# Second attention of a two-layer transformer: searches and sort one slot on with three near buffers, and ScalarE's exponential between its two counts

## The reference, cut to what matters

```
B, T, D, H = x.shape[0], 1024, 128, 16      # as run: x is (4, 1024, 128)
topk = max(1, int(Tx * 0.3))
scale = Dx ** (-0.5)
...
scores = jnp.einsum('bhid,bhjd->bhij', q, k) * scale
topk_scores, indices = jax.lax.top_k(scores, topk)
...
masked = jnp.full_like(scores, -jnp.inf)
masked = masked.at[bi, hi, ti, indices].set(topk_scores)
attn = jax.nn.softmax(masked, axis=-1)
out = jnp.einsum('bhij,bhjd->bhid', attn, v)
```

## Time and profile before

| | |
|---|---|
| median of 3 runs | 3562.24 us (3561.92 to 3563.55) |
| the profiled execution | 3559.1 us |
| its span | 3557.4 us |
| busy share of the span: PE, DVE, ACT, POOL | 77%, 76%, 70%, 56% |
| mean granted TensorE clock | 0.787 of full speed |
| second attention, about | 1050 us to 3120 us of the span |

### The profile page before, as it was taken

How to read it: one execution, slowest core, us unless ns; L and a number is a source line. 1 busy time by engine, 2 the same in 40 slices (tenths; PEclk the granted TensorE clock), 3 DMA queues, 4 the chain that set the end, 5 groups by cost and what they waited for, 6 DMA issues and landing times. The chain is left out here.

```text
span 3557.4 us, 74747 instructions
## 1 busy us (share of the span) xinstructions
PE 2733.3 (77%) x23705; PEld 1525.9 (43%) x23705; DVE 2690.0 (76%) x8588; ACT 2479.6 (70%) x4051; POOL 1983.9 (56%) x4543
## 2 busy tenths in 40 slices
PE   4699999677745777777777776776777777757999
PEld 2233333233423445454444454453445545444444
DVE  5787787235439989999999989897999999834444
ACT  2266666433128999999999999997999999822222
POOL 3133333410228888888888888886888888730000
PEclk8699999888655777777777778777777777777999
DMA  5211221000230101101101100110110110010000
GB/s 154 78 52 46 52 52 32 12 27 21 73 55 1 14 5 17 16 3 17 17 2 17 17 11 8 17 15 3 17 14 5 17 17 2 2 31 0 9 6 9
DMA packets 115265, 85.88 MB, mean 24 GB/s; under 512 B 58153, under 2 KB 97339, under 8 KB 114875
## 3 DMA queue, kind: packets, MB, share of 16 engines
q1 hardware_dynamic: 106331, 75.20, 9.8%
q0 software_dynamic: 8192, 4.79, 0.9%
q10 hardware_dynamic: 352, 1.18, 0.1%
HBM read 54.25 MB, written 19.40 MB: 21 GB/s over the span
## 5 line engine op out<-in xcount | busy, mean ns | idle before, releaser
L1285 POOL TENSOR_TENSOR a_near<-a_side,a_z 128x1024 int32<-128x1024 int32 x512 | 968.3, 1891 | 42.8
L1181 PE MATMUL a_ST<-a_qs,a_ks 75*128 75x128 bf16 x4096 | 732.9, 267 | 304.7 <-ACT a_eT L1220 210.7
L1381 DVE MAX8 a_cand<-a_near 128x8 f32<-128x256 f32 x2048 | 752.5, 412 | 4.7 <-POOL a_near L1285 4.7
L1181 PEld LDWEIGHTS a_ST<-a_qs,a_ks 75*128 75x128 bf16 x4096 | 496.8, 123 | 507.5 <-issue 500.2
L1417 DVE TENSOR_SCALAR_CACHE_REDUCE a_z<-a_S,a_thr 128x1024 f32<-128x1024 f32 x512 | 649.7, 1269 | 75.2 <-issue 54.2
L1205 ACT ACTIVATE a_signs<-a_z,a_tiny 128x1024 bf16<-128x1024 f32 x512 | 590.2, 1153 | 96.8 <-DVE a_z L1417 95.9
L1198 ACT ACTIVATE a_signs<-a_S,search 128x1024 bf16<-128x1024 f32 x512 | 573.6, 1120 | 22.7 <-PE a_S L1134 22.6
L1220 ACT ACTIVATE a_eT<-a_ST 128x1024 f32<-128x1024 f32 x512 | 523.1, 1022 | 71.8 <-PE a_ST L1182 70.0
L775 ACT ACTIVATE a_eT<-a_ST 128x512 f32<-128x512 f32 (+3 forms) x768 | 354.1, 489 | 212.2 <-PE a_ST L745 152.2
L1134 PE MATMUL a_S<-a_ks,a_qs 72*128 72x512 bf16 x1024 | 431.9, 515 | 83.8 <-DVE a_z L1417 60.9
L879 DVE TENSOR_REDUCE a_mx<-a_S 128x1 f32<-128x512 f32 (+3 forms) x768 | 380.8, 547 | 92.3 <-PE a_S L732 55.9
(11 more groups left out here) (342 smaller groups left out, 4451.2 us busy)
## 6 DMA issues: line engine op xcount, KB each, us to landing
a_qs<-q_parts SPq DMA_DIRECT2D x174, 64.0 KB
a_ks<-k_parts SPq DMA_DIRECT2D x174, 64.0 KB
a_qs<-a_flip SPq DMA_DIRECT2D x512, 0.8 KB
q_parts<-p_qp SPq DMA_DIRECT2D x48, 128.0 KB, 1.8
k_parts<-p_kp SPq DMA_DIRECT2D x48, 128.0 KB, 1.8
a_qs<-q_parts SPq DMA_DIRECT2D x60, 96.0 KB
a_ks<-k_parts SPq DMA_DIRECT2D x60, 96.0 KB
f_w<-L_ffn_W SPq DMA_DIRECT2D x16, 256.0 KB, 2.9
```

Source lines behind the costliest of these rows:

```text
L1181: pe.matmul(ST[:, block_of], ks[:, base(hl) + kb * P:base(hl) + (kb + 1) * P], qs[:, tile(hl):tile(hl) + P], start=True, stop=False)
L1285: pool.tensor_tensor(near[:, hl % 2, :].bitcast(I32), side[:, one].bitcast(I32).broadcast_to([P, SEQ]), z[:, hl % H, :].bitcast(I32), ALU. ...
L1381: mm = dve.max(found[:, 8 * g:8 * g + 8], near[:, h2 % 2, g * SW:(g + 1) * SW])
```

## The change

Three things change. First, `near` has three buffers instead of two, `TOPL` becomes 3 and `SORT` 4: VectorE searches and sorts a tile one slot later, and GpSimd may write `near` of tile l when the searches of tile l - 3 are done. The transposition of the split maxima keeps its slot under a name of its own (`FLIPL`). Second, the working row of the fallback path (`general`, `selection`) takes no buffer of its own any more but a slice of `z`. Third, ScalarE takes the exponential directly behind count 1, ahead of count 2 and of the mask.

```diff
-    MASKS, RING = 4, 8
+    MASKS, RING, NEARS = 4, 8, 3
...
-        near = sb("near", [P, 2, SEQ])
-        tied = near[:, 0, :]
+        near = sb("near", [P, NEARS, SEQ])
...
-        C2, TOPL, SORT, HIT, CUTL, CHECK, PICK = 1, 2, 3, 5, 6, 7, 15
+        C2, FLIPL, TOPL, SORT, HIT, CUTL, CHECK, PICK = 1, 2, 3, 4, 5, 6, 7, 15
...
                     act.activation(signs[:, 0, :], S[h % 2][:, :], ACT.Sign, bias=first[:, bass.ds(n, 1)],
                                    accum_out=sgn[0][:, one]).then_inc(cnt1, 1)
+                if lagged(it, h, TURN, UN, TOTAL) is not None:
+                    l, hl = nth(it, h, TURN), here(h, TURN)
+                    act.wait_ge(turned, l + 1)
+                    if not (isinstance(it, int) and l < RING):
+                        act.wait_ge(pv, it * QU + (h - TURN) // 4)
+                    act.activation(eT[:, hl % RING, :], ST[:, :], ACT.Exp, scale=SCALE1).then_inc(e_done, 1)
...
                     act.activation(mask[:, hl % MASKS, :], z[:, hl % H, :], ACT.Relu, bias=cut_steep[:, hl % H:hl % H + 1],
                                    scale=-STEEP).then_inc(mask_a, 1)
-                if lagged(it, h, TURN, UN, TOTAL) is not None:
-                    l, hl = nth(it, h, TURN), here(h, TURN)
-                    act.wait_ge(turned, l + 1)
-                    if not (isinstance(it, int) and l < RING):
-                        act.wait_ge(pv, it * QU + (h - TURN) // 4)
-                    act.activation(eT[:, hl % RING, :], ST[:, :], ACT.Exp, scale=SCALE1).then_inc(e_done, 1)
...
-                    if not (isinstance(it, int) and l < 2):
-                        pool.wait_ge(top_s, l - 1)
-                    pool.tensor_tensor(near[:, hl % 2, :].bitcast(I32), side[:, one].bitcast(I32).broadcast_to([P, SEQ]),
+                    if l >= NEARS:
+                        pool.wait_ge(top_s, l - (NEARS - 1))
+                    pool.tensor_tensor(near[:, hl % NEARS, :].bitcast(I32), side[:, one].bitcast(I32).broadcast_to([P, SEQ]),
...
-                                general(j, here(h, CHECK + 7), group)
+                                general(j, here(h, CHECK + 7), group, near[:, here(h, TOPL) % NEARS, :], z[:, h % H, :])
```

More of the change, by code:

```diff
@@ L1027, in attention1 @@
         idle = sb("idle", [1, 2 * H])
-        work, last8, half = sb("work", [P, SEQ]), sb("last8", [P, 8]), sb("half", [P, 1])
+        last8, half = sb("last8", [P, 8]), sb("half", [P, 1])
         more, ties, lack, upto8 = sb("more", [P, 1]), sb("ties", [P, 1]), sb("lack", [P, 1]), sb("upto8", [P, 8])
@@ L1304, in _, with selection @@
             dve.wait_ge(const, 1)
-            def selection(zj):
-                dve.tensor_copy(work[:, :], zj)
+            def selection(zj, work):
+                dve.tensor_copy(work, zj)
                 dve.drain()
                 with dve.Fori(0, ROUNDS):
-                    dve.max(last8[:, :], work[:, :])
+                    dve.max(last8[:, :], work)
                     dve.drain()
-                    dve.match_replace(work[:, :], last8[:, :], work[:, :], GONE)
+                    dve.match_replace(work, last8[:, :], work, GONE)
                     dve.drain()
-                dve.max(last8[:, :], work[:, :])
+                dve.max(last8[:, :], work)
                 dve.drain()
@@ L1318, in selection, with general @@
                 dve.drain()
-                dve.match_replace(work[:, :], last8[:, :], work[:, :], GONE)
+                dve.match_replace(work, last8[:, :], work, GONE)
                 dve.drain()
-                dve.tensor_scalar(work[:, :], work[:, :], GONE, None, ALU.is_le)
+                dve.tensor_scalar(work, work, GONE, None, ALU.is_le)
                 dve.drain()
-            def general(j, h0, group):
+            def general(j, h0, group, tied, work):
                 flag = dve.value_load(flags[0:1, bass.ds(j, 1)].bitcast(I32), min_val=0, max_val=2 ** 31 - 1)
@@ L1330, in general @@
                     at = cut[:, bass.ds(h0 % H + j, 1)]
-                    dve.tensor_scalar(work[:, :], zj, at, None, ALU.is_gt, ALU.add, accum_out=more[:, :])
+                    dve.tensor_scalar(work, zj, at, None, ALU.is_gt, ALU.add, accum_out=more[:, :])
                     dve.tensor_scalar(tied, zj, at, None, ALU.is_equal, ALU.add, accum_out=ties[:, :])
@@ L1345, in general @@
                     dve.drain()
-                    dve.scalar_tensor_tensor(work[:, :], tied, 2.0, work[:, :], ALU.is_equal, ALU.add)
+                    dve.scalar_tensor_tensor(work, tied, 2.0, work, ALU.is_equal, ALU.add)
                     dve.tensor_scalar(fail[:, 0:1], fit[:, 2:3], -1.0, 1.0, ALU.mult, ALU.add)
@@ L1360, in general @@
                     with dve.If(still > 0):
-                        selection(zj)
-                    dve.tensor_copy(zj, work[:, :])
+                        selection(zj, work)
+                    dve.tensor_copy(zj, work)
                     dve.tensor_copy(at, half[:, :])
@@ L1380, in top @@
                     if has2 is not None:
-                        mm = dve.max(found[:, 8 * g:8 * g + 8], near[:, h2 % 2, g * SW:(g + 1) * SW])
+                        mm = dve.max(found[:, 8 * g:8 * g + 8], near[:, h2 % NEARS, g * SW:(g + 1) * SW])
                         if g == SEGS - 1:
@@ L1448, in slot @@
                 elif h % 2:
-                    if lagged(it, h, TOPL, UN, TOTAL) is not None and ends(h, TOPL):
-                        q, ring = quad(it, h, TOPL), ((h - TOPL) // 4) % 2
+                    if lagged(it, h, FLIPL, UN, TOTAL) is not None and ends(h, FLIPL):
+                        q, ring = quad(it, h, FLIPL), ((h - FLIPL) // 4) % 2
                         dve.wait_ge(part_s, PART_STEPS * q + PART_STEPS)
```

## The result

The changed kernel takes 3896.2 us (median of 4 runs, 3895.42 to 3907.54) against 3562.08 us: ratio 1.0945, with a 95% interval of 1.0924 to 1.0965. It is slower, 14 us inside the upper end of the stated range (3665 to 3910), and some 100 us beyond the predicted 3800. First the page of the profile after, with span and busy shares.

What follows compares the result with a forecast made beforehand. ScalarE comes first, with waits between close engines deciding. Per eight slots, 29.44 + 2.92 + 0.38 + 2.75 = 35.49 us against 31.79, +236 us over 63.9 groups: 3798, stated as 3800 us, range 3665 to 3910.

Steps and rivals of the forecast that it cites:

- the reckoned mix: Main case, TensorE's turns partly at half and partly at full clock: 3798 us, own range 3690 to 3890, chance 0.63.
- the rival with the half clock: Rival: TensorE runs at half clock throughout, +392 us, 3954 us, chance 0.15.
- odd slots: ScalarE's exponential waits for a turn needing the mask just made: 0.73 us each, 2.92 us in eight slots.
- slot 2: ScalarE's exponential waits for TensorE's scores, product and turn after the previous exponential: 0.38 us, bounds 0 to 1.27.
- slot 6: ScalarE's exponential waits for a turn behind TensorE's check, which waits for `ctx` and `z`: 2.75 us.
- The clock, a share of 0.56 at half: TensorE's mean clock of 0.72 read as a 0.56 share of time at half clock, making a turn 1.54 us.
- the bounds: Full- to half-clock waits per eight slots: odd slots 1.12 to 4.32, slot 2 0 to 1.27, slot 6 2.61 to 2.89 us.
- the start of `z`: VectorE starts `z` 0.24 us after `thr1` starts: 0.19 for `thr1`, 0.05 for the hand-over.
- The chain that the prediction follows from X: From count 2 in slot 4 (X) to slot 5's `z` at X + 5.74 and slot 6's exponential at X + 9.86.
- the contention for GpSimd's `near`: A `near` beside VectorE's mask in slot 5 takes 0.55 us longer, bounds 0 and 0.75.
- All 2.35 us of waits removed: ScalarE's existing waits in eight slots all vanish, 31.79 down to 29.44 us, 150 us in all.
- The signs named: Profile marks expected: `near` waits gone, turn wait some 390 us, TensorE waiting for the mask, clock within 0.05 of 0.72.

Runs made afterwards that it cites:

- x2: The kernel before with only the exponential moved ahead of count 2: 3915.0 us, ratio 1.1002.
- x1: The changed kernel with the exponential put back behind the mask, so only later searches and sort with three near buffers: 3490.8 us, ratio 0.9809.
- x3: The changed kernel with the turn, and the product, copy, transposition and norm after it, at later lags (turn two slots later): 3808.0 us.
- x4: The changed kernel with TensorE's check matmul moved behind the turn of its slot: 3698.9 us.
- x8: The changed kernel with TensorE's score matmuls done twice in every slot, with the same result: 3914.2 us.
- x10: The changed kernel with GpSimd writing near one slot later, directly behind thr1 of its slot: 3783.2 us.
- x6: The kernel of x1 with TensorE's check behind the turn: 3479.7 us, ratio 0.9769 to the kernel before.
- x5: The changed kernel with both the turn two slots later and the check behind the turn: 3695.4 us.
- x11: The changed kernel with the turn two slots later, the check behind the turn and near written one slot later on GpSimd: 3708.3 us.
- x9: The kernel of x1 with GpSimd writing near one slot later, directly behind thr1 of its slot: 3699.4 us.

## Why the prediction was right, and where it was off

**Direction and mechanism: right.** x2 and x1 divide the change: the moved exponential costs 356 us by itself and the near part gains 68. The waits stand where the prediction put them, behind the odd masks (x3 removes those of slots 5, 7 and 1) and behind the check (x4 takes 197 us off). But 3896 us lies just outside the 3690 to 3890 of the reckoned mix, towards the rival with the half clock, so the sum needs an account of its own. Measured as the prediction reckons, from the start of count 1 to that of the exponential less 1.09, and averaged over the trace from 1150 us on, in us for eight slots:

| term | forecast | measured |
|---|---|---|
| odd slots | 2.92 | 3.41 |
| slot 2 | 0.38 | 0.49 |
| slot 6 | 2.75 | 3.74 |

Together this is 1.6 us more in eight slots, 100 us in 63.9 groups, which is the distance from 3798 to 3896.

**Odd slots, 0.73 us each.** Measured 0.85 each. A shown turn lasts 1.88 us (from 1503.31 to 0.04 before 1505.23), the half-clock figure, and its exponential comes 1505.23 - 1503.15 - 1.09 = 0.99 late. The term was too small by the clock: with the granted 0.58 the share of time at half clock is 0.84, not 0.56. It stays below 1.08, the bound at half clock, since the turn follows the mask by 0.05 and not 0.15 us, and since some odd slots do not wait at all.

**The clock, a share of 0.56 at half.** The prediction's two sums were 3798 us for 0.56 and 3954 for all at half clock; between them, 0.84 gives 3798 + 0.28 / 0.44 x 156 = 3897 us, and 3896 was measured. That agreement is luck. The same step between the bounds gives 3.81, 0.95 and 2.84 us for the three terms, too much for the first two and too little for the third. The mean clock of the earlier trace rows was taken over into another schedule; it belongs to the schedule. The rival with the clock spoke for this side, and its page ("TensorE: Matmul & The Clock Gate" of the Trainium skill, Part 1: activity lifts the throttled default) agrees in direction with 0.72 falling to 0.58 here and with the rise to 0.63 in x8. A longer slot by itself does not lower the clock, though: x3 and x10 have nearly the same pace (4.48 and 4.44 us a slot), but clocks of 0.71 and 0.63 (columns of the earlier trace rows, x3 first):

```profile
1100.00:3000.00 1900.00, 1260.60 (x14427) 791.64 (x14425) 1742.85 (x5443) 1576.75 (x2420) 1384.63 (x3368) 0.71 0.08 11
```

```profile
1100.00:3000.00 1900.00, 1435.85 (x14597) 902.81 (x14596) 1552.89 (x5498) 1605.91 (x2443) 1371.69 (x3399) 0.63 0.08 11
```

**Slot 6, 2.75 us.** Measured 3.74, beyond even its bound of 2.89 at half clock: this is the term that was mis-sized most. The clock is not the reason, since at half clock both the turn and ScalarE, by its own wait in slot 5, come some 0.3 us later. The step that failed is the start of `z`, put 0.24 us behind that of `thr1`. The chain that the prediction follows from X, in the rows ahead of the shown slot 6 (X is the first row's start):

```profile
1489.03 1.16 ACT L1210 ACTIVATE a_signs<-a_z,a_tiny 128x1024 bf16<-128x1024 f32 x1
...
1491.78 1.89 POOL L1284 TENSOR_TENSOR a_near<-a_side,a_z 128x1024 int32<-128x1024 int32 x1
...
1492.93 1.29 DVE L1461 TENSOR_SCALAR a_mask<-a_z,a_cut 128x1024 bf16<-128x1024 f32 x1
...
1493.63 0.64 POOL L1287 TENSOR_TENSOR a_rank<-a_sgn,a_shifted 128x1 f32<-128x1 f32 x1
...
1494.49 0.19 POOL L1260 TENSOR_TENSOR a_thr<-a_scaled,search 128x1 f32<-128x1 f32 x1
...
1495.56 1.26 DVE L1416 TENSOR_SCALAR_CACHE_REDUCE a_z<-a_S,a_thr 128x1024 f32<-128x1024 f32 x1
...
1498.14 0.29 PE L1180 MATMUL a_ST<-a_qs,a_ks 75*128 75x128 bf16 x1
```

`thr1` starts at X + 5.46, where 5.50 was reckoned. That is partly luck: the `near` was not stretched by 0.55, but the small step behind it took 0.64 instead of 0.19. `z` starts at X + 6.53 instead of X + 5.74, and from there to the turn it is 2.58, as reckoned (2.54). In between VectorE was not free: its mask took 1.29 us instead of 0.75, and its searches stand behind it. In the 57 groups of eight from slot 46 to slot 494 `z` always starts 0.87 or 0.88 us behind the end of `thr1`. The prediction priced the contention for GpSimd's `near` alone and put VectorE's side of it, and VectorE's own queue, at nothing. Two pairs of rows of the changed kernel show what happens:

```profile
1512.17 2.46 POOL L1284 TENSOR_TENSOR a_near<-a_side,a_z 128x1024 int32<-128x1024 int32 x1
...
1520.45 1.89 POOL L1284 TENSOR_TENSOR a_near<-a_side,a_z 128x1024 int32<-128x1024 int32 x1
```

```profile
1512.14 0.75 DVE L1461 TENSOR_SCALAR a_mask<-a_z,a_cut 128x1024 bf16<-128x1024 f32 x1
...
1520.49 2.41 DVE L1461 TENSOR_SCALAR a_mask<-a_z,a_cut 128x1024 bf16<-128x1024 f32 x1
```

The one that starts second waits most of the first out. A `near` 0.03 us behind a mask takes 0.57 longer, as reckoned. But a mask 0.04 us behind a `near` takes 1.66 longer, and the prediction had no such case. Masks make up half of VectorE's added busy time and two small instructions the rest, as these lines of the changed kernel give (instructions, busy time, mean):

```profile
L1461 DVE TENSOR_SCALAR a_mask<-a_z,a_cut 128x1024 bf16<-128x1024 f32 x254 | 358.4, 1411 | 1.2 <-PE a_ST L1181 1.2
L1427 DVE TENSOR_TENSOR a_hits<-a_odd,a_rank 128x64 f32<-128x64 f32 x128 | 113.6, 888 | 0.1
L1442 DVE TENSOR_TENSOR a_signals<-a_cand,a_edge 128x16 f32<-128x16 f32 x128 | 113.3, 885 | 0.0
```

Before, they took 190.7, 28 and 21 us; all of VectorE rose by 325. Contention is not what makes the whole loss, though: x2 and x10 have next to none (masks of 0.753 and 0.758 us on average), with the exponential between the counts, and lose 356 and 226 us.

**All 2.35 us of waits removed.** Nearly so in the changed kernel: ScalarE's wait for `z` is 30.2 us, 14.0 of it one wait on the fallback path. It is too much said for the near part by itself, which gains 68 us of the 150; x1 still shows 71.4 us of waiting for `z`. The check holds some of the rest, and x6 recovers 11 us of it.

**The signs named.** Waits for `near` gone: right. Wait for the turn 390 us: 441, with 194 of it in odd slots. TensorE waits for the mask: right. A `near` of 2.4 us or more: 18 of 512, up to 2.469. The wait of slot 6 between 2 and 3 us: wrong, 3.5. The clock within 0.05 of 0.72: wrong. The turn 0.15 us behind the mask's end: 0.05 in the shown rows.

**Open.** What the lower clock costs by itself (x8 changed it too little), and why x5 and x11 stay at some 3700 us with the waits behind mask and check cut. Their rows point to VectorE and `z`. How much of the gain of x10 is the missing contention and how much the earlier `thr1` is open too, as is what sets the granted clock of a stage.

## What to carry to other kernels

In an in-order pipeline, count what stands between a producer and the consumer of its product's product: the exponential depended on the mask through TensorE, and its move left one instruction as cover for a 1.1 to 1.9 us turn. Measure the two halves of a combined change apart: here one was worth 1.9% and the other cost 10%. Before an engine is freed of a wait, ask what that wait kept apart: here it kept VectorE's masks away from GpSimd's `near`. And in a chain over several engines an instruction starts when its input is there and its own engine is free; check both.

## What the runs showed of the hardware

VectorE's mask (fp32 in, bf16 out, 128x1024) and GpSimd's `near` nearly exclude each other, in both directions: 0.75 to 2.41 us and 1.89 to 2.46. In the changed kernel 128 masks start while a `near` runs, up to 1.7 us into it, and every one of them ends 0.54 to 0.56 us behind the end of that `near`. Tiny instructions pay the same: `hits` (128x64, two inputs) went from 0.223 to 0.888 us on average, `signals` (128x16) from 0.162 to 0.885. The searches (0.41 us) and `z` (1.27 us) beside the same `near` kept their time. How the instructions fall decides: moving `near` by one slot cost 209 us in x9, where more of them fell together, and gained 113 in x10, where they came apart, with no instruction more.

The granted clock of a stage is not a property of its work: with the same matmuls it was 0.73 before, 0.57 in the changed kernel, 0.63 in x10 and 0.71 in x3 (1100 to 3000 us), the last two at nearly the same pace.
